# A two-layer decoder on one core: two of its three phases merged into one list of work, their order made anew, and one score product laid out differently

## The reference

```python
x = ln(x + attention0(x))            # 16 heads of 16, causal, a bias by distance on the logits
x = ln(x + cross_attention0(ctx, x)) # 16 heads, 64 keys a batch
x = ln(x + experts(x))               # 2 shared + the 2 best of 8 routed: (silu(x@w1)*(x@w3))@w2, hidden 128
x = ln(x + attention1(x))            # q, k, v = x @ w_lat @ w_heads, 16 heads of 16, causal
qh = x @ Wq + bq; kh = ctx @ Wk + bk; vh = kh @ Wv + bv      # cross attention 1, one head of 256
s = where(mask == 0, -10000, qh @ kh.T)
x = ln(x + softmax(s) @ vh @ Wo + bo)
x = ln(x + relu(q(x @ W1 + b1)) @ W2 + b2)    # q: an elementwise function with a sine, width 1024
```

## Time and profile before

| what | us |
|---|---|
| median of 3 runs (3622.93 to 3631.72) | 3624.59 |
| the profiled execution | 3628.03 |
| its span in the trace | 3626.1 |
| PE busy in the span | 3344.5 (92%) |
| DVE busy | 2625.4 (72%) |
| ACT busy | 2283.5 (63%) |
| POOL busy | 1022.4 (28%) |

### The profile page before, as it was taken

One profiled execution on the slowest core, in us unless ns is written; L12 is line 12 of the kernel. 1 busy time (PEld: TensorE's weight loads), 2 busy tenths in 40 slices (PEclk: granted clock), 3 DMA queues, 4 the chain that ended last, 5 costly groups with the idle time before them and its releaser, 6 DMA issues.

```text
span 3626.1 us, 59862 instructions
## 1 busy us (share of the span) xinstructions
PE 3344.5 (92%) x20706; PEld 2528.1 (70%) x20706; DVE 2625.4 (72%) x7153; ACT 2283.5 (63%) x4067; POOL 1022.4 (28%) x1576
## 2 busy tenths in 40 slices
PE   5999999999999848999999999999999876999998
PEld 4677777777777636777777777777777655766664
DVE  5688888888888644677777777777777534788876
ACT  3677777777777622456666555556556543677776
POOL 2244444444444422222222322222223110000000
PEclk8999999999999979999999999999999877999999
DMA  7654545445544021444444444444444421011010
GB/s 193 101 95 84 88 96 107 84 88 95 107 84 82 17 82 53 84 80 77 86 92 94 94 88 88 90 89 93 92 87 88 73 44 62 12 36 35 25 35 24
DMA packets 203403, 283.27 MB, mean 78 GB/s; under 512 B 48929, under 2 KB 131874, under 8 KB 194274
## 3 DMA queue, kind: packets, MB, share of 16 engines
q1 hardware_dynamic: 203106, 279.46, 38.2%
HBM read 179.49 MB, written 96.73 MB: 76 GB/s over the span
## 4 chain that ended last, share of the span: by engine, by line
PE 71%; ACT 11%; DVE 7%; DMA 5%; issue 4%; SPq 1%; POOL 1%; PEld 0%; POOLq 0%; ACTq 0%; PEldq 0%; DVEq 0%
PE ps L829 35%; PE ps L1003 8%; PE ps L978 7%; PE ps L1201 5%; PE ps L1017 5%; ACT q_stack L1669 5%; PE ps L953 3%; DMA qk_scratch<-parts 3%; ACT pt L1686 2%; PE ps L984 1%; PE ps L1077 1%; PE ps L888 1%; PE ps L1028 1%; DMA k_stack<-qk_scratch 1%; DVE nmax L1351 1%
## 5 line engine op out<-in xcount | busy, mean ns | idle before, releaser
L1686 ACT ACTIVATE pt<-ps 128x512 f32<-128x512 f32 x1280 | 735.9, 598 | 346.7 <-PE ps L1003 338.8
L1889 POOL TENSOR_SCALAR_AFFINE_SELECT pt<-pt 128x256 f32<-128x256 f32 x1024 | 392.1, 419 | 704.9 <-ACT pt L1686 704.9
L978 PE MATMUL ps<-k_stack,q_stack 96*128 96x512 f32 (+3 forms) x2048 | 547.2, 338 | 42.3 <-ACT q_stack L1669 11.8
L1358 DVE CUSTOM_DVE_ANT_0 ps<-ps,future 128x512 f32<-128x512 f32 (+3 forms) x1024 | 481.7, 515 | 141.9 <-PE ps L978 138.8
L1003 PE MATMUL ps<-q_stack,k_stack 100*128 100x512 f32 (+3 forms) x2048 | 538.6, 345 | 29.3 <-ACT q_stack L1669 23.4
L1003 PEld LDWEIGHTS ps<-q_stack,k_stack 100*128 100x128 f32 x2048 | 351.5, 195 | 124.9 <-ACT q_stack L1669 37.2
L978 PEld LDWEIGHTS ps<-k_stack,q_stack 96*128 96x128 f32 x2048 | 355.6, 194 | 103.2 <-ACT q_stack L1669 18.8
L1351 DVE TENSOR_REDUCE nmax<-ps 128x1 f32<-128x512 f32 (+2 forms) x768 | 354.4, 502 | 92.0 <-PE ps L984 91.0
L1895 POOL TENSOR_TENSOR rs<-rs 128x4 f32<-128x4 f32 x96 | 97.1, 1012 | 1062.0 <-DVE rs L1394 1062.0
L1669 ACT ACTIVATE q_stack<-ps 4x512 fp32r<-4x512 f32 x512 | 300.8, 588 | 64.7 <-PE ps L992 56.5
L1017 PE MATMUL ps<-pt,v_ones 128*32 128x512 f32 (+3 forms) x4096 | 312.1, 446 | 5.7 <-POOL pt L1889 5.3
(11 more groups left out here) (278 smaller groups left out, 7958.6 us busy)
## 6 DMA issues: line engine op xcount, KB each, us to landing
qk_scratch<-parts SPq DMA_DIRECT2D x64, 1024.0 KB, 5.5
q_stack<-qk_scratch SPq DMA_DIRECT2D x384, 128.0 KB, 4.9
k_stack<-qk_scratch SPq DMA_DIRECT2D x384, 128.0 KB, 5.6
gate_of<-gate_scratch SPq DMA_DIRECT2D x128, 256.0 KB, 5.6
x_mid<-x_ring SPq DMA_DIRECT2D x32, 512.0 KB, 3.9
x_ring<-x_mid SPq DMA_DIRECT2D x32, 512.0 KB, 5.3
x_ring<-in_x SPq DMA_DIRECT2D x16, 512.0 KB, 3.8
out_dram<-x_ring SPq DMA_DIRECT2D x16, 512.0 KB, 2.9
```

The costliest lines, as they stand in the source:

```text
L978: done = e.matmul(bank(bank_of[piece])[:, at:at + width], a.q[0:96, base + h, t * P:(t + 1) * P], a.k[0:96, base + h, 0:width], start=a.la ...
L1358: done = e.tensor_tensor_reduce(src, src, future[:, SEQ - width:SEQ], -1.0, 3e38, ALU.add, ALU.min, nmax[:, g % 2, to:to + 1])
L1686: e.activation(dst, src, ACT.Exp).then_inc(exp_up.sem)
L1889: done = e.affine_select(out=blk, in_=blk, compare_op=ALU.is_ge, fill=0.0, base=0, pattern=[[0, 2], [1, P]], channel_multiplier=-1)
```

## The change

**One list for phases 1 and 2.** Phase 2's table gets a start (`START[2]`, 1179.5), and both phases' pieces are sorted together, without barrier, prologue or the 44 matmuls of warming up in it. The last attention of phase 1 (batch 15) and its cross attention now stand among the first experts: on PE the first expert product follows `S 15.3.3`. The weights come one pair of experts at a time: 5 DMAs (786 KB each) from SP into the place of the score stacks, as soon as the last `T` that reads the place is done; ACT copies the high part (1536 columns) and DVE subtracts (1536 columns). Other new pieces (`AHEAD`): `rt` (router), `low` and `lw` (the low-rank product: 6 times 3 matmuls, an ACT copy and a DVE split of 256 columns), `wo`, and `z` (the stacks of attention 1 cleared: two DVE and two POOL memsets of 96x2048, two ACT copies). They stand behind `tm xw 15`. SBUF is laid out by hand (`skip`) so that all this fits, and the two attentions share v, pt, oh, ol, oT, o and rec; the experts' `bk` shares oT, which adds a wait on ACT between `O` and `bk` (`copy_before`). The 108 warm matmuls by `WARM` stay.

**New table.** The periods written down change from 70.45, 91.45 and 31.45 to 71.238, 90.623 and 31.852 and all offsets with them. In the steady part of phase 1 the order is the same on all engines but PE (117 of a period's 123 pieces keep theirs), in phase 3 on all engines. In phase 2, 125 of 145 pieces keep their place on PE, 68 of 86 on ACT, 67 of 87 on DVE.

**cs as one unit.** High and low parts of the keys lie side by side (`a_parts`), so that one matmul of 128 columns takes both: 4 matmuls a token tile instead of 6. DVE copies one half out of PSUM (128x256) and adds it. `q_bias` is folded into the mask's offset once in prologue 3 (4 DVE operations of 128x512 more, ACT's 2 copies less), and bo is added by POOL (`tb x1`: 128x1024) instead of by the matmuls of one row.

```diff
-    1: (70.45, {
+START = {1: 0.0, 2: 1179.5, 3: 0.0}
+    1: (71.238, {
...
-    2: (91.45, {
+    2: (90.623, {
...
+AHEAD = {
+    "tensor": {"lw": [1237.1, 1237.2, 1237.3, 1237.4, 1237.5, 1237.6]},
+    "scalar": {"w2": [1114, 1129, 1141, 1145, 1157], "rt": [1100], "low": [1161],
...
+    "gpsimd": {"z": [1237, 1240]},
+    "sync": {"w2": [1106, 1121, 1134.5, 1134.6, 1150], "rt": [1090], "low": [1154], "wo": [1241]},
+}
...
-        for ph in (1, 2, 3):
+        for ph, part in ((1, 12), (3, 3)):
             for engine in ENGINES:
                 first = [("ld", ph, b) for b in range(RING)] if engine == "sync" else []
-                rest = [piece for piece in turns[ph][engine] if piece not in first]
+                rest = [piece for piece in turns[part][engine] if piece not in first]
                 walk[engine] += first + [("prologue", ph)] + rest + [("end", ph)]
...
-                if kind == "prologue" and key[0] == 2:
-                    e.wait_ge(w_lo.sem, W3_READY - len(W3.chunks) - 2)
-                    warm(bank(7)[:, 0:P], 20)
...
+                elif kind == "lw":
+                    which, c = key[0] // CT, key[0] % CT
+                    e.wait_ge(*ahead_lo["low", 0])
...
+                    product(e, bank(bank_of[piece])[:, 0:DIM], three(
+                        low_h[:, 0, rows], low_l[:, 0, rows], low_h[:, 1, cols], low_l[:, 1, cols])).then_inc(lw_up.sem)
...
                 elif kind == "up":
                     b, i, which = key
-                    w = (w1, w3)[which]
                     e.wait_ge(*tc_lo["ex", b])
+                    if b == 0:
+                        e.wait_ge(*ahead_lo["w2", i // 2])
...
-                    ops.append((ones[:, :], co_b[:, :]))
...
                 elif kind == "cs":
...
                     for t in range(TT):
                         rows = slice(t * P, (t + 1) * P)
-                        ops = []
-                        for c in range(CT):
-                            ops += three(ch[:, c, rows], cl[:, c, rows], a_h[:, c, keys], a_l[:, c, keys])
-                        done = product(e, bank(bank_of[piece])[:, t * CTX:(t + 1) * CTX], ops)
+                        both = bank(bank_of[piece])[:, 2 * t * CTX:2 * (t + 1) * CTX]
+                        done = None
+                        for c, part in ((0, ch), (0, cl), (1, cl), (1, ch)):
+                            wide = part is ch
+                            done = e.matmul(both if wide else both[:, 0:CTX], part[:, c, rows],
+                                            a_parts[:, c, b, :, :].rearrange("p a k -> p (a k)") if wide else a_parts[:, c, b, 0, :],
+                                            start=wide and c == 0, stop=wide and c == 1)
                     done.then_inc(cs_up.sem)
...
+                        for n in range(2):
...
+                            e.tensor_tensor(tile32[:, n, :], bank(4 + n), seen[:, cols], ALU.mult).then_inc(mine.up())
+                            e.wait_ge(*mine.now)
+                            e.tensor_tensor(offset[:, cols], offset[:, cols], tile32[:, n, :], ALU.add).then_inc(mine.up())
...
+                elif kind == "w2":
+                    i, = key
+                    cols = slice(i * 2 * PER_EXPERT, (i + 1) * 2 * PER_EXPERT)
+                    e.wait_ge(*ahead_hi[piece])
+                    e.tensor_tensor(w2_l[:, cols], w2_raw[:, cols], w2_h[:, cols].bitcast(F32),
+                                    ALU.subtract).then_inc(ahead_lo.sem)
...
+                elif kind == "z":
+                    e.wait_ge(*tm_up["xw", BATCH - 1])
+                    e.memset(att[1].rows(0, key[0])[0:96, :, :].bitcast(F32), 0.0).then_inc(ahead_lo.sem)
...
-                    e.tensor_tensor(sc3[:, :, :], bank(bank_of[piece])[:, 0:TT * CTX].rearrange("p (t k) -> p t k", t=TT),
-                                    key_row(q_bias), ALU.add).then_inc(cs_add.sem)
+                    halves = bank(bank_of[piece]).rearrange("p (t a k) -> p t a k", t=TT, a=2)
+                    e.tensor_copy(sx3[:, :, :], halves[:, :, 1, :]).then_inc(mine.up())
+                    e.wait_ge(*mine.now)
+                    e.tensor_tensor(sc3[:, :, :], halves[:, :, 0, :], sx3[:, :, :], ALU.add).then_inc(cs_add.sem)
...
-                    if group_before(n, g, 1):
-                        e.wait_ge(*o_turned[group_before(n, g, 1)])
+                    if piece in copy_before:
+                        before = copy_before[piece]
+                        e.wait_ge(*(o_turned[before[1:]] if before[0] == "O" else bk_up[before[1:]]))
...
+                    i, = key
+                    cols = slice(i * 2 * PER_EXPERT, (i + 1) * 2 * PER_EXPERT)
+                    group = ((i + 1) * 2 * PER_EXPERT - 1) // (GROUP * SEQ)
+                    e.wait_ge(*t_up[BATCH - 1, group, UNITS - 1])
+                    e.dma_start(w2_raw[:, cols], dram["w2"][:, cols]).then_inc(w2_in[i], 16)
```

More of the change, by code:

```diff
@@ L1 @@
+import itertools
 from contextlib import ExitStack
@@ L114, in __init__, with only, marks @@
         self.until = dict.fromkeys(banks, -1e9)
-        self.left = {}
+        self.left, self.mine = {}, list(banks)
+    def only(self, banks):
+        part = Banks(banks)
+        part.until, part.left, part.mine = self.until, self.left, list(banks)
+        return part
+    def marks(self, banks):
+        out = []
+        for bank in banks:
+            if bank in self.left and self.left[bank] not in out:
+                out.append(self.left[bank])
+        return out
     def take(self, mark, until, n=1):
-        firsts = [bank for bank in self.until if bank + n - 1 in self.until and (n == 1 or bank % 2 == 0)]
+        firsts = [bank for bank in self.mine if bank + n - 1 in self.mine and (n == 1 or bank % 2 == 0)]
         first = min(firsts, key=lambda bank: max(self.until[bank + i] for i in range(n)))
@@ L443, in pieces_of, with ahead_of, merged @@
     return out
+AHEAD = {
[8 rows of a table added]
+}
+SPLIT_AHEAD = ("w2", "rt", "low", "lw", "wo", "z")
+def ahead_of(engine):
+    return {(kind, i): at for kind, row in AHEAD[engine].items() for i, at in enumerate(row)}
+EDGE = {engine: {} for engine in ENGINES}
+def merged(when):
+    out = {engine: {**when[1][engine], **ahead_of(engine), **when[2][engine]} for engine in ENGINES}
+    for piece, at in out["gpsimd"].items():
+        if False:
+            out["gpsimd"][piece] = max(at, out["vector"].get(piece, at))
+    for engine in ENGINES:
+        out[engine].update(EDGE[engine])
+    return out
 def times_of(ph):
@@ L457, in times_of @@
                 if row and row[n] is not None:
-                    out[engine][piece] = b * period + row[n]
+                    out[engine][piece] = START[ph] + b * period + row[n]
     return out
@@ new lines, in low_tiles, with landing @@
+        def low_tiles(n):
+            return [sb(st2, f"w_tile{next(spare)}", [P, DIM], F32R) for _ in range(n)]
+        def landing(name, shape):
+            with ExitStack() as here:
+                return sb(here, name, shape)
+        w2_h = sb(st2, "w2_hi", [P, ALL * PER_EXPERT], F32R)
+        tiles = low_tiles(2)
+        w2_raw = landing("w2_raw", [P, ALL * PER_EXPERT])
+        w2_l = sb(st2, "w2_lo", [P, ALL * PER_EXPERT], F32R)
+        tiles += low_tiles(5)
+        skip(320)
+        gate_of = sb(st2, "gate_of", [P, 2, SEQ])
@@ new lines, in decoder @@
+        att[1].k = [k1_first, sb(st2, "k_stack1b", [P, GROUP, SEQ], F32R)]
+        tiles += low_tiles(4)
+        wo_raw = landing("wo_raw", [P, CT, DIM])
+        tiles += low_tiles(2)
+        st2.close()
+        att[1].share(att[0])
+        back2 = [back2_first, att[1].oT]
+        lgT = back2_first[0:EXPERTS, :]
+        w_low = [[[tiles[(part * 3 + which) * CT + c] for c in range(CT)] for which in range(3)] for part in range(2)]
+        wo1 = [[tiles[12 + part * CT + c] for c in range(CT)] for part in range(2)]
@@ L904, in tensor @@
                         product(e, bank(q), ops).then_inc(kt_up)
-                elif kind == "prologue" and key[0] == 2:
-                    e.wait_ge(low_parts, 2)
-                    for which in range(3):
-                        for c in range(CT):
-                            rows = slice(which * DIM + c * P, which * DIM + (c + 1) * P)
-                            cols = slice(which * DIM, (which + 1) * DIM)
-                            product(e, bank(which * CT + c)[:, 0:DIM], three(
-                                low_h[:, 0, rows], low_l[:, 0, rows],
-                                low_h[:, 1, cols], low_l[:, 1, cols])).then_inc(low_up)
                 elif kind == "prologue" and key[0] == 3:
@@ L1125, in tensor @@
                     b, i, c = key
-                    cols = slice(c * P, (c + 1) * P)
                     e.wait_ge(*h3_lo[b, i])
                     if i == 0:
-                        for free in left[piece]:
+                        for free in left.get(piece, ()):
                             e.wait_ge(*free)
```

(8 more changed lines are left out.)

509 lines of the change are left out of this document (304 added, 205 removed), and 266 rows, old and new, of tables (AHEAD, TABLE).

## The result

| | median of 8 runs | lowest to highest |
|---|---|---|
| before | 3624.6 us | 3622.5 to 3631.7 |
| after | 3641.3 us | 3633.8 to 3660.6 |

The ratio is 1.0048 (95% interval 1.0031 to 1.0066). 3508 was forecast. The profiled execution of after has a span of 3638.2 us, 12.1 more than that of before.

What follows compares the result with a forecast made beforehand. PE was taken to bound the three loops, with stalls at the seam between phases 1 and 2. Terms −74 − 24 − 21 + 3 = −116 took the profiled 3628.0 to 3512, 3508 as median; range 3466 to 3562.

Steps and rivals of the forecast that it cites:

- What bounds the kernel: Whole kernel: PE sets the time of the three loops; the rest is at the seam between phases 1 and 2.
- Steady phase 2, −24: 14 periods from S 17.0.0: hid_l wait goes, 1.7 us saved a period, −24 us; bounds −49 and +8.
- rival for the other side: Steady phase 2, slower than before: attention and experts wait for each other on ACT through O and bk; chance 3%.
- its 3644: Total time in us if the ring of O and bk on ACT cost 8 us a period in phase 2.
- upper bound of +8: Steady phase 2's worst end: waits only change names and one more of 0.6 us a period comes, +8 us.
- Phase 1, 0 ± 9: Phase 1 keeps its order but for six pieces on PE, which is 97% busy: 0, ±9 us.
- Seam, −74: S 15.0.0 to S 17.0.0: experts fill PE's stalls, 414.3 us becomes 340, −74; ends −40 and −98.
- the edge behind `z`: Behind tm xw 15: memsets and six lw splits take 6 us, mostly hidden by 14 us of expert pieces; 20 in all.
- Its own signs: At the seam, between 1150 and 1500 on PE: no gap over 3 us and no clock under 0.9.
- Phase 3, −1.5 a batch: Phase 3 on PE: eight fewer score matmuls −0.89, no one-row bo matmuls −0.62; −1.5 us a period, −21 in all.
- POOL's addition of bo: Rival in phase 3: POOL's addition holds DVE, at worst 2.4 us a batch, 38 in all, giving 3546; chance 5%.
- Prologue 3, +3: Prologue 3: four added DVE operations of 0.64 us each before the barrier that waits for DVE, +3 us.

Runs made afterwards that it cites:

- banks_v0: The kernel after, with the PSUM banks of some cross attention pieces pinned for batches 0 to 13, so tm v0 takes its old banks: 3626.9 us, ratio 1.0009.
- before_tmv_wait: The kernel before, with one wait added: on PE tm v0 also waits until DVE has read xs 7 of batch b-2: 3648.6 us, ratio 1.0061.
- old_bo: The kernel after with rows 2 loaded before the gate load, tm v0's old banks, and bo again by two one-row matmuls: 3565.7 us, ratio 0.9834.

## Why the prediction was wrong, step by step

The forecast missed by 133 us. Of the 128 that the stretches account for, 72 are steady phase 2, 33 the seam, 19 phase 1 and 6 phase 3, with 2 the other way at its prologue.

- **What bounds the kernel.** Right: PE's queue sets the loops, and what PE waits for is what the changes move.
- **Steady phase 2, −24. This step failed.** It looked at hid_l, ACT and DVE, and at those it was right: with SP's two pieces in the old order the period is 94.2, −1.4 against the forecast −1.7. But it priced no move on SP. The prediction says "what is late next is the score tile whose maxima now stand 0.7 later, and two bank releases"; late next was a load, which PE waits for 3.2 us a batch, and behind that wait the clock takes 1.3 more, which no term had either. Its rival for the other side named an `O` and `bk` ring and asked for over 6.6 us a period. That its 3644 lies near the measured 3641 is luck: the ring did not show, the true wait cost 4.5, and that was enough because the seam gave 33 us less than forecast and phase 1 lost 19. The order of SP showed the gate load ahead of the rows, at a place where SP issues seven loads in 3.3 us. The upper bound of +8 for the term was wrong by 40 us.
- **Phase 1, 0 ± 9. Failed**, +19. The loop that it spoke of, in the kernel before:

```profile
471.20:979.30 508.10, 492.87 (x3690) 373.12 (x3686) 432.85 (x1024) 388.05 (x700) 228.50 (x357) 1.00 0.51 93
```

  That it "keeps its order but for six pieces" was true of PE and not enough: the same table assigns the banks, and a bank's last reader is a wait that no order shows. banks_v0 and before_tmv_wait put 1.1 to 1.3 us a batch on it; 0.4 stays open.
- **Seam, −74.** The mechanism was right and the size off: −41. Attention 15 to `tm p0 15` took 123.2 where 110.5 was said, cross attention 82.2 (77.5), up to `S 16.0.0` 72.6 (59), the last part 95.2 (93). The step that was mis-sized most is the one behind `tm xw 15`: the prediction hid most of the edge behind `z` and counted the trip of q and k through DRAM as unchanged. PE's waits there are 4.8 us for w_tile, 6.1 for hid_l and 6.2 for the first k_stack, and the granted clock is 0.85. Its own signs, no gap over 3 us and no clock under 0.9, failed there. PE's waits in the seam, the four largest:

```profile
PE ps L1110 <- DMA k_stack<-qk_scratch: 8.3, 2, 6.2
PE ps L1135 <- ACT pt L1870: 6.1, 4, 2.8
PE ps L964 <- DVE w_tile L1477: 4.8, 4, 1.8
PE ps L964 <- DVE hid_l L1670: 4.6, 3, 3.1
```

  DVE is not the limit in attention 15 that I took it for: it is busy 85.3 of 107.5 there, and taking 9 us off it brought some 3. ACT's exponentials (pt) are PE's largest wait in attention 15. Warming up, put at 22 us in PE's queue, was worth 8 in the median and 10 to 16 in the seam.
- **Phase 3, −1.5 a batch.** −1.2. The slots of 0.111 held: 16 matmuls of `cs` in 1.74 us, whatever their columns. From the timeline of PE, after:

```profile
3187.67 0.22 PE L1298 MATMUL ps<-a_parts,xh 128*128 128x128 f32 x1
3187.73 0.36 PE L1298 MATMUL ps<-a_parts,xl 128*128 128x64 f32 x2
...
3189.41 2.79 PE L1338 MATMUL ps<-act,w_down 128*128 128x512 f32 x6
```

  (3189.41 − 3187.67)/16 = 0.109 us for 128 columns and for 64, against the 0.111 of the earlier trace rows. The two bo matmuls were worth 0.63 (old_bo), forecast 0.62. 0.3 a batch of the forecast did not come: the slot ahead of `bk` is 0.3 longer, the one from `fd 2` to `fa 6` 0.5 longer with 0.3 less right behind it, and the profile names no releaser; this is open. DVE's extra copy was covered, as forecast. The formula by columns, given for an isolated matmul, in "TensorE: Matmul & The Clock Gate" of the Trainium skill, section "Back-to-back issue gap", would have given nothing here; P/1.2 in its section "LDWEIGHTS (loading the stationary operand)" fits again.
- **POOL's addition of bo.** The rival did not come true in the steady loop: taking the addition out (old_bo) changes the period by PE's 0.63 and no more. Whether it costs at phase 3's start is open.
- **Prologue 3, +3.** Nothing to be seen: +0.8 together with the end of phase 2, a stretch that scatters by 5 us (172.6 to 177.9) between the profiles of the new kernels.

On the gate load: it was issued first and the rows landed 2.6 to 2.7 us later. The Trainium skill's "DMA: Bandwidth & Descriptors", section "Queues, rings and completion order", says that on each DMA engine descriptors are consumed in ring order. The landings agree with that rule.

## What to carry to other kernels

When a table or a planner is re-made, compare the order of the queue that only issues DMAs first, pair by pair, wherever two loads are issued within a landing time of each other: one swap there cost three times what the rest of the new order gained. The same holds for what the table decides besides the order: list for each PSUM bank its last reader before and after. And where several terms of a sum are each small per batch, put a bound on every queue, the idle-looking ones too. A stall of PE of some 3 us is not priced by its length alone: look at the granted clock of the stretch behind it.
